# Turned keys of two of four score chunks: loaded from HBM, or turned on TensorE

## The reference

```python
x1 = layernorm(modality1, ln1_g, ln1_b)
x2 = layernorm(modality2, ln2_g, ln2_b)     # the context
q = x1 @ Wq + bq
k = x2 @ Wk + bk
v = x2 @ Wv + bv
scores = jnp.einsum('bqe,bke->bqk', q, k) * scaling
attn = jax.nn.softmax(scores, axis=-1)
ctx = jnp.einsum('bqk,bke->bqe', attn, v)
return ctx @ Wo + bo
```

## Time and profile before

| | us |
|---|---|
| median of 3 executions | 670.63 (665.77 to 671.51) |
| the profiled execution | 672.1 |
| its span, first to last instruction | 670.4 |
| TensorE busy | 606.7 (91%) |
| VectorE busy | 410.6 (61%) |
| ScalarE busy | 260.2 (39%) |
| GpSimd busy | 195.8 (29%) |
| cross attention, from the first turned key to the last weighted tile | 44 to 314 |

### The profile page before, as it was taken

One profiled execution on the slowest core, in us unless ns is written; L12 is line 12 of the kernel. 1 busy time (PEld: TensorE's weight loads), 2 busy tenths in 40 slices (PEclk: granted clock), 3 DMA queues, 4 the chain that ended last, 5 costly groups with the idle time before them and its releaser, 6 DMA issues.

```text
span 670.4 us, 13550 instructions
## 1 busy us (share of the span) xinstructions
PE 606.7 (91%) x5333; PEld 385.4 (57%) x5333; DVE 410.6 (61%) x1004; ACT 260.2 (39%) x627; POOL 195.8 (29%) x259
## 2 busy tenths in 40 slices
PE   5999979999999999998768799999999899998777
PEld 4655445545555555543537395866758585675545
DVE  3974588787778679725567481735548282645522
ACT  0322343757566543532112251533515162351412
POOL 0323387696867775630000000101010000101010
PEclk8999999999999999999788799999999999999879
DMA  8953455464777554729042303021030303012000
GB/s 293 368 184 118 148 201 162 136 189 154 238 237 259 160 190 155 245 107 365 20 115 106 96 1 96 18 80 33 23 88 2 95 18 95 19 56 57 1 17 17
DMA packets 46175, 83.11 MB, mean 124 GB/s; under 512 B 19472, under 2 KB 22048, under 8 KB 44064
## 3 DMA queue, kind: packets, MB, share of 16 engines
q1 hardware_dynamic: 46112, 82.24, 37.7%
HBM read 71.75 MB, written 10.49 MB: 123 GB/s over the span
## 4 chain that ended last, share of the span: by engine, by line
PE 55%; issue 29%; DVE 7%; ACT 4%; POOL 2%; DMA 1%; SPq 0%; DVEq 0%; POOLq 0%; ACTq 0%
PE u_ps L816 10%; PE s_ps L790 9%; PE bank L772 6%; PE bank L878 4%; PE s_ps L772 3%; PE bank L958 2%; PE s_ps L683 2%; ACT area L551 2%; PE u_ps L934 2%; PE bank L988 2%; PE max_ps L958 2%; PE s_ps L716 2%; PE bank L965 1%; DVE area L1318 1%; PE bank L905 1%
## 5 line engine op out<-in xcount | busy, mean ns | idle before, releaser
L461 POOL TENSOR_SCALAR area<-area 128x384 f32<-128x384 f32 (+1 forms) x160 | 106.7, 678 | 10.3 <-POOL area L454 10.3
L1052 DVE BATCH_NORM_STATS2 area<-area 128x6 f32<-128x384 f32 (+1 forms) x208 | 104.0, 541 | 0.0
L551 ACT COPY area<-bank 128x384 f32<-128x384 f32 (+1 forms) x139 | 61.7, 480 | 68.9 <-PE bank L772 68.8
L454 POOL TENSOR_TENSOR area<-area,minus_half 128x4 f32<-128x4 f32 (+1 forms) x56 | 57.1, 1020 | 82.0 <-DVE area L1061 81.5
L816 PE MATMUL u_ps<-area,yT_all 128*64 128x384 f32 (+1 forms) x416 | 78.6, 499 | 0.0
L497 POOL TENSOR_TENSOR area<-area,minus_half 128x1 f32<-128x1 f32 x8 | 4.3, 538 | 242.4 <-DVE area L1312 242.4
L772 PE MATMUL bank<-ident_f,area 128*128 128x128 f32 (+1 forms) x417 | 63.3, 275 | 3.9 <-ACT area L551 2.5
L790 PE MATMUL s_ps<-area 128*64 128x512 f32 x288 | 66.0, 594 | 0.0
L772 PEld LDWEIGHTS bank<-ident_f,area 128*128 128x128 f32 (+1 forms) x417 | 45.1, 141 | 28.4 <-issue 17.6
L934 PE MATMUL u_ps<-area 128*128 128x512 f16 x256 | 60.7, 387 | 0.0
L1152 DVE TENSOR_REDUCE area<-s_ps 128x1 f32<-128x512 f32 x24 | 16.6, 690 | 56.2 <-PE s_ps L790 56.2
(11 more groups left out here) (173 smaller groups left out, 1033.0 us busy)
## 6 DMA issues: line engine op xcount, KB each, us to landing
area<-in_ctx_dram SPq DMA_DIRECT2D x96, 384.0 KB, 3.9
area<-in_L_ffn_W_turned_dram SPq DMA_DIRECT2D x16, 1024.0 KB, 7.9
skew<-area SPq DMA_DIRECT2D x8, 1024.0 KB, 3.9
area<-skew SPq DMA_DIRECT2D x16, 256.0 KB, 4.6
x_sb<-in_x_dram SPq DMA_DIRECT2D x8, 256.0 KB, 9.0
out_dram<-area SPq DMA_DIRECT2D x8, 256.0 KB, 2.0
area<-in_ctx_dram SPq DMA_DIRECT2D x16, 97.5 KB
area<-n_L_xattn_Wq_turned_dram SPq DMA_DIRECT2D x1, 1024.0 KB, 6.9
```

Of the source, the lines that this page charges most:

```text
L454: pool.tensor_tensor(rs[b][:, sl], ve[b][:, sl], minus_half[:, 0:n], ALU.pow).then_inc(s["rstd_ready"], 1)
L461: pool.tensor_scalar(raw[b][0:m, u, j, :], raw[b][0:m, u, j, :], negmu[b][0:m, i:i + 1], rs[b][0:m, i:i + 1], ALU.add, ALU.mult).then_inc( ...
L551: act.copy(xT[c % 2][:, u, :, (j % CH) * P:(j % CH) * P + m], tbank[i % 3][:, 0:KC * P].rearrange("p (c k) -> p c k", c=KC)[:, :, 0:m]).th ...
L1052: dve.bn_stats(st[b][0:m, stat_at(u, j), :], raw[b][0:m, u, j, :]).then_inc(s["key_stats_done"], 1)
```

## The change

The host lays out a second copy of the context, `ctx_turned`: for each batch 384 rows (width) of 1024 keys, those of chunks 1 and 2, not normalised. `load_given` brings one chunk of both batches into `xT`, 1.57 MB in 2 DMAs; chunk 2's waits for the same pair's chunk 0 to be scored, whose buffer it takes, chunk 1's for the previous pair's chunk 1. Tiles 4 to 11 are not turned and not copied. The statistics and the normalising of `raw` stay. The mean is dealt with by centring `a_sb` over the width once (`mean` on TensorE, `centre` on VectorE, in pair 0); the reciprocal deviation of each key is spread over the 64 query rows of its batch by `spread_factors` (8 matmuls with the identity), copied to SBUF by `factors_out`, and multiplied onto the scores in PSUM in the same instruction that takes the maximum. The third turning bank becomes the bank of the factors; two banks are left for turning. The tail has its own buffer. The factors live in the buffer of `fb2`, whose load moves behind the last maximum. The `xvo` groups of pair 0 move two tiles later, behind two `mean` groups.

```diff
+    GIVEN = (1, 2)
+    TURNED = [j for j in range(NJ) if j // CH not in GIVEN]
-        yw, _ = carve(at - 2 * KC * CH * P * 4, [P, D])
+        yw = fb2
+        xT_tail, at = carve(at, [P, 2, KC, TAIL])
+        factors = fb2
-        EXTRA |= {KC + i: ("xvo", i) for i in range(XVO_ROW + 1)}
+        EXTRA |= {KC + h: ("mean", h) for h in range(2)}
+        EXTRA |= {KC + 2 + i: ("xvo", i) for i in range(XVO_ROW + 1)}
-        tbank = [bank[0], bank[1], s_ps[:, 1536:2048]]
+        tbank = [bank[0], bank[1]]
+        factors_bank = s_ps[:, 1536:2048]
+        def slot(ch):
+            return xT_tail if ch == NCH - 1 else xT[ch % 2]
 # SyncE
+            def load_given(p, ch):
+                at_least(sp, s["chunk_scored"], NCH * (p - 1) + 2 if ch == 1 else NCH * p + 1)
+                i = GIVEN.index(ch)
+                for u in range(2):
+                    sp.dma_start(xT[ch % 2][:, u, :, :], A["ctx_turned"][2 * p + u].rearrange("(c d) k -> d c k", d=P)[:, :, i * CH * P:(i + 1) * CH * P]
+                                 ).then_inc(given_loaded[i], 16)
             for k in range(NL):
                 load_pair(0, k)
+            load_given(0, 1)
...
-            for k in range(NL):
+            for k in range(3):
                 load_pair(1, k)
+            load_given(0, 2)
+            for k in range(3, NL):
+                load_pair(1, k)
+            load_given(1, 1)
...
+            load_given(1, 2)
             for p in range(2, NP):
                 for k in range(NL):
                     load_next(p, k)
+                    if k == 2:
+                        load_given(p, 1)
                     if p in (4, 5) and k in (2, 5):
                         load_for_sum(2 * p - 4 + (k - 2) // 3)
+                load_given(p, 2)
...
+            sp.wait_ge(s["chunk_max"], NCH * NP)
+            sp.dma_start(fb2, A["L0_ffn_b2"].partition_broadcast(P)).then_inc(s["fb2_loaded"], 16)
 # ScalarE
-                at_least(act, s["chunk_scored"], c - 1)
+                at_least(act, s["chunk_scored"], NCH * (p - 1) + 3 if j < FT else NCH * p)
+            def factors_out(p, ch):
+                i = len(GIVEN) * p + GIVEN.index(ch)
+                act.wait_ge(s["factors_ps"], i + 1)
+                at_least(act, s["chunk_max"], NCH * p + 2 if ch == GIVEN[1] else NCH * (p - 1) + 3)
+                act.copy(factors, factors_bank).then_inc(s["factors_copied"], 1)
...
-                            evacuate(p, j)
+                            if j in TURNED:
+                                evacuate(p, j)
...
+                    if p < NP and b in (3, 5):
+                        factors_out(p, GIVEN[(b - 3) // 2])
                     if 0 <= q < NP and b in (1, 3, 5, 6):
                         pt_out(q, (1, 3, 5, 6).index(b))
 # TensorE
+                elif kind == "mean":
+                    pe.wait_ge(s["a_ready"], KC + i + 2)
+                    for c in range(KC):
+                        ins = pe.matmul(dst[:, :], ones_f[:, :], a_sb[:, c, i * 512:(i + 1) * 512], start=(c == 0), stop=(c == KC - 1))
+                    ins.then_inc(s["mean_ps"], 1)
...
-                    at_least(pe, s["turned_copied"], i - 2)
+                    at_least(pe, s["turned_copied"], i - 1)
+            def spread_factors(p, ch):
+                i = len(GIVEN) * p + GIVEN.index(ch)
+                if i == 0:
+                    pe.wait_ge(s["cq_sums"], NT)
+                pe.wait_ge(s["rstd_ready"], NB * p + 2 * ch + 2)
+                at_least(pe, s["factors_copied"], i)
+                for j in range(CH):
+                    for u in range(2):
+                        at = stat_at(u, CH * ch + j)
+                        ins = pe.matmul(factors_bank[u * L:(u + 1) * L, j * P:(j + 1) * P], rs[p % 2][:, at:at + 1].to_broadcast([P, L]),
+                                        ident_f[:, :], start=True, stop=True)
+                ins.then_inc(s["factors_ps"], 1)
...
-                            turn(p, j)
+                            if j in TURNED:
+                                turn(p, j)
...
+                        if b in (3, 5):
+                            spread_factors(p, GIVEN[(b - 3) // 2])
 # VectorE
+            def centre(h, src):
+                dve.wait_ge(s["mean_ps"], h + 1)
+                for c in range(KC):
+                    dve.scalar_tensor_tensor(out=a_sb[:, c, h * 512:(h + 1) * 512], in0=src[:, :], scalar=-1.0 / DC, in1=a_sb[:, c, h * 512:(h + 1) * 512],
+                                             op0=ALU.mult, op1=ALU.add).then_inc(s["a_centred"], 1)
...
-                dve.tensor_reduce(mx[:, ch:ch + 1], score_of(ch), AX.X, ALU.max).then_inc(s["chunk_max"], 1)
+                if ch in GIVEN:
+                    dve.wait_ge(s["factors_copied"], len(GIVEN) * p + GIVEN.index(ch) + 1)
+                    dve.tensor_tensor_reduce(score_of(ch), score_of(ch), factors, 1.0, -3.0e38, ALU.mult, ALU.max, mx[:, ch:ch + 1]).then_inc(s["chunk_max"], 1)
+                else:
+                    dve.tensor_reduce(mx[:, ch:ch + 1], score_of(ch), AX.X, ALU.max).then_inc(s["chunk_max"], 1)
```

The host part:

```diff
+    laid["ctx_turned"] = given["ctx_768"][:, :keys * P, :].reshape(-1, P, keys, given["ctx_768"].shape[2])[:, :, 4:12, :].transpose(0, 3, 2, 1).reshape(
+        given["ctx_768"].shape[0], given["ctx_768"].shape[2], 8 * P)
```

More of the change, by code:

```diff
@@ L251, in build_program @@
         raw_loaded = [[sem(f"raw_loaded{b}{k}") for k in range(NL)] for b in range(2)]
+        given_loaded = [sem(f"given_loaded{c}") for c in GIVEN]
         x_loaded = [sem(f"x_loaded{h}") for h in range(2)]
@@ L373, in _ @@
                 sp.dma_start(relT[h * DH:(h + 1) * DH, :], A["L0_attn_rel_emb_turned"][:, first_rel:first_rel + REL]).then_inc(s["rows_loaded"], 16)
-            for dst, key in ((xbo, "xattn_bo"), (abo, "attn_bo"), (fb2, "ffn_b2")):
+            for dst, key in ((xbo, "xattn_bo"), (abo, "attn_bo")):
                 sp.dma_start(dst, A["L0_" + key].partition_broadcast(P)).then_inc(s["rows_loaded"], 16)
+            load_given(1, 2)
             for p in range(2, NP):
@@ L542, in evacuate @@
             def evacuate(p, j):
-                c, m = NCH * p + j // CH, P if j < FT else TAIL
-                if c == 1:
+                m = P if j < FT else TAIL
+                if p == 0 and j == TURNED[1]:
                     act.wait_ge(s["cq_sums"], NT)
-                at_least(act, s["chunk_scored"], c - 1)
+                at_least(act, s["chunk_scored"], NCH * (p - 1) + 3 if j < FT else NCH * p)
                 for u in range(2):
-                    i = 2 * (NJ * p + j) + u
+                    i = 2 * (len(TURNED) * p + TURNED.index(j)) + u
                     act.wait_ge(s["key_turned"], i + 1)
-                    act.copy(xT[c % 2][:, u, :, (j % CH) * P:(j % CH) * P + m],
-                             tbank[i % 3][:, 0:KC * P].rearrange("p (c k) -> p c k", c=KC)[:, :, 0:m]).then_inc(s["turned_copied"], 1)
+                    act.copy(slot(j // CH)[:, u, :, (j % CH) * P:(j % CH) * P + m],
+                             tbank[i % 2][:, 0:KC * P].rearrange("p (c k) -> p c k", c=KC)[:, :, 0:m]).then_inc(s["turned_copied"], 1)
+            def factors_out(p, ch):
[3 more added lines that the diff above has]
+                act.copy(factors, factors_bank).then_inc(s["factors_copied"], 1)
             def exps(q, part):
@@ L786, in scores @@
                     pe.wait_ge(s["xvo_taken"], WO_OUT + XVO_ROW)
-                pe.wait_ge(s["turned_copied"], 2 * (NJ * p + min(CH * (ch + 1), NJ)))
+                if ch in GIVEN:
+                    pe.wait_ge(given_loaded[GIVEN.index(ch)], 32 * (p + 1))
+                else:
+                    pe.wait_ge(s["turned_copied"], 2 * len(TURNED) * p + (2 * CH if ch == 0 else 2 * len(TURNED)))
                 for c in range(KC):
@@ L1238, in _ @@
                             weights(1, EXTRA[j][1], (u_ps, max_ps)[j % 2])
+                        if p == 0 and j in EXTRA and EXTRA[j][0] == "mean":
+                            centre(EXTRA[j][1], (u_ps, max_ps)[j % 2])
                     if p == SMALL_AT and b == 4:
@@ L1403 @@
     laid["L0_attn_rel_emb_turned"] = turned(given["L0_attn_rel_emb"][::-1])
+    keys = given["ctx_768"].shape[1] // P
+    laid["ctx_turned"] = given["ctx_768"][:, :keys * P, :].reshape(-1, P, keys, given["ctx_768"].shape[2])[:, :, 4:12, :].transpose(0, 3, 2, 1).reshape(
+        given["ctx_768"].shape[0], given["ctx_768"].shape[2], 8 * P)
     laid["columns"] = turned(_np.concatenate([given["L0_" + name].reshape(-1, P) for name in
```

24 lines of the change are left out of this document (12 added, 12 removed).

## The result

| | before | after |
|---|---|---|
| median of the executions | 669.70 us (665.77 to 671.51) | 681.03 us (676.61 to 682.55) |
| ratio | | 1.0166 [1.0098, 1.0234] |
| the profiled execution | 672.1 | 680.11 |
| its span | 670.4 | 678.4 |
| its mean TensorE clock | 0.959 | 0.945 |

I had forecast 655.5 us, in a range of 646 to 668.

What follows compares the result with a forecast made beforehand. TensorE was taken to bound each pair (29.69 of 30.20 us busy). Six periods falling from 30.2 to 28.0 give 13.2, plus 3.0 in pair 7, less 1.1 in pair 0: 15.1 us off, so 655.5 us, range 646 to 668.

Steps and rivals of the forecast that it cites:

- Work on TensorE: Cross-attention pairs: 6.6 us of turning removed, about 1.0 us of spreading added in each of chunks 1 and 2.
- rival 2: Spreading in each pair costs its upper bound of 1.9 us; period 29.1, about 665 us, no change; chance 0.14.
- the lost cover: Before the turned context, removing tiles 4 and 5 exposes TensorE's wait for ScalarE's copy, so A shrinks only 0.4 us.
- The load delays VectorE: Next pair's tile 0 lands at S0 + 7.8 behind the turned load; VectorE waits 2.4 us in pairs 1 to 6.
- The chain behind the wait: After VectorE's wait: chunk 1's maximum at S0 + 9.3, then factor copy, then third probability copy done at 11.2.
- Idle 0.75 us: TensorE, arriving at 10.5 after the tail tile, idles 0.75 us for ScalarE's third probability copy.
- No clock term: TensorE's clock was full at 25.1 of 29 us busy, so nothing was added for a slower clock.
- The first (no delay, 648.6): The turned load in SyncE's queue delays nothing; period 26.85, 648.6 us; chance 0.18.
- The third (half rate, 681 us): Turned load at half rate or less makes VectorE's loop the bound; 669 us at 200 GB/s, 681 at 160; chance 0.12.

Runs made afterwards that it cites:

- e1_order: Changed kernel with the next pair's tiles 0 and 1 requested ahead of chunk 2's turned load: 654.73 us, 0.9767 of the kernel before.
- e2_act_first: Changed kernel with ScalarE's probability copy put ahead of its factor copy: 680.38 us, 1.0147 of the kernel before.
- e8_spread_xvo: Changed kernel with tiles 0 and 1 ahead of the turned load, probability copy ahead of factor copy, pair 0's xvo groups spread over later tiles: 651.3 us.
- e12_half_bias: Changed kernel with chunk 2's turned load halved from pair 1 on and GpSimd's bias additions moved behind the pair loop: 661.79 us, 0.99 of before.
- e4_filler: Changed kernel with 20 identity transposes put into TensorE's idle time in each of pairs 1 to 5: 672.81 us, 1.0034 of before.
- e13_weights_apart: Changed kernel with both orders (loads, ScalarE copies) swapped, bias additions late, xvo spread, third turning bank, two weight pieces moved into pair 3: 645.98 us.
- e5_half: Changed kernel with chunk 2's turned load cut to 256 of 512 columns from pair 1 on: 681.88 us, 1.0196 of the kernel before.

## Why the prediction was wrong, step by step

- **Work on TensorE: right.** Spreading takes 1.04 us, step 0.98 (I took 1.0; rival 2, 1.9, fell). The second turned tile of a block waits 0.39 us for one of the two banks (0.37). The turned context waits 0.68 for ScalarE, as the lost cover said. Chunk 0 to chunk 1 is 6.8 us of TensorE against 7.0, pair 7 gave 3.1 us against 3.0, pair 0 cost 1.6 against 1.1.
- **The load delays VectorE: right, and mis-sized.** I had tile 0 at S0 + 7.8. It landed at S0 + 9.5 (request at 166.3, 7.8 us to landing) and the wait is 3.91 us, not 2.4. The rate was not the error: from 167.0 on the queues moved 394 GB/s, where I had taken 393.

```profile
164.85:174.10 9.25, 9.25 (x76) 4.78 (x72) 5.28 (x18) 3.25 (x6) 6.62 (x10) 1.00 0.87 315
...
167.00:174.10 7.10, 7.10 (x54) 3.32 (x50) 3.14 (x13) 1.98 (x4) 5.64 (x8) 1.00 1.02 394
```

  From the request of the turned load (164.85) to the landing of tile 0 (174.1) that is 2.91 MB, and the turned load with tiles 0 and 1 is 2.36 MB. The other 0.55 MB can only belong to the tile requests behind, which were being served while tile 0 was incomplete; at 394 GB/s it takes 1.4 us, nearly the whole miss of 1.5. I had let the queue finish one load before it began the next. This is an estimate from the bytes; no run isolates it. The Trainium skill (DMA: Bandwidth & Descriptors, section Bandwidth) states about 358 GB/s per core on the HBM side; here the trace does not agree, with 394 over 7 us.
- **The chain behind the wait: right in order, missing a collision.** I had the maximum at S0 + 9.3; it came at S0 + 11.56: 1.5 from the load, 0.5 from `own_norm` under GpSimd's additions (1.00 instead of 0.47), 0.2 not accounted for. I had looked at GpSimd only for its sum (22.8 of 28 us) and not for what its 2.5 us of additions do to a VectorE instruction beside them. In this pair they end at 176.07 and `own_norm` at 176.28:

```profile
173.58 2.49 POOL L503 TENSOR_TENSOR x_sb<-x_sb,area 128x512 f32<-128x512 f32 x2
```

- **Idle 0.75 us: wrong, 3.2, and the first step that failed.** The maximum late by 2.3 passes on in full, since nothing on the chain has slack. With pair 6, where TensorE idles 4.84 us behind small reductions that I had not looked at, this is 15.7 us over the six pairs.
- **"No clock term": wrong, and the second step that failed.** I argued from a window with TensorE busy 25.1 of 29 us at clock 1.00. That was an average, and its longest single idle stretch was 1.46 us, half of what my own chain came to make:

```profile
88.89 0.55 PE L772 MATMUL s_ps<-ident_f,area 128*128 128x128 f32 x3 [1.46 <-DVE area L1146]
```

  What the engine did before the clock fell is one stretch of idle time. In the cross attention of all the kernels here, behind each stretch of 2.41 us and more it went to half speed. Shorter ones went either way: half speed behind 1.40 (e1_order) and 2.01 to 2.12 (e2_act_first), full speed behind 1.40 (e8_spread_xvo), 1.46 (before), 2.15 (e12_half_bias) and 2.17 (pair 1 of after). I had a priced idle stretch in my own chain and asked only for its length. Some 12.4 us in the trace, 8 by e4_filler for pairs 1 to 5.
- **Rivals.** The first (no delay, 648.6) is about what e1_order tests: 654.7, since TensorE and VectorE then wait for each other and most periods stay at 28 us or more. With its collisions and the banks mended (e13_weights_apart) three of six periods are 26.2, the others 26.8 to 28.0. The third (half rate, 681 us) names the measured time, but by luck: the turned load ran at full rate, 394 GB/s. Its form, VectorE's loop as the bound, isn't seen either: VectorE was busy under 23 of each 29 us.
- **Range and chances.** The lower and upper ends came from the price of the load and of the spreading. Nothing in it stood for an idle stretch longer than the 0.75 us, or for what one does to TensorE afterwards, so 13 us above the upper end was outside every case.

## What to carry to other kernels

When a change makes TensorE wait once a round, price the wait twice: its length, and the groups behind it at half clock. A trace in which the clock stayed behind much shorter stretches is no reason to leave the second price out. A new load belongs behind whatever the next stage wants first in the same queue, even when both fit the period; here that was a difference of 26 us. And when removing one cause gives nothing, look at what took up the time gained before calling it innocent: e5_half alone would have cleared the load, wrongly.

## What the runs showed of the hardware

- **Half clock after a short wait.** Idle stretches of 2.41 to 3.70 us ahead of a weighted group were followed each time by 1.2 GHz for about 3 to 7 us of work (a weighted group of 1.51 us takes 2.83), which costs 1.4 to 2.9 us in the pairs measured. Between 1.40 and 2.30 us it went either way. 20 transposes in the gap, 2.35 us of them, kept 2.4 GHz and made the kernel 8 us faster.
- **GpSimd's additions stop some VectorE instructions entirely.** While GpSimd adds two 128x512 f32 tiles (2.49 us), a VectorE `tensor_scalar` with operands in SBUF ends only when both are done: 0.47 became 1.94 to 3.10 us, 0.17 became 2.73. The statistics of a tile beside the same additions took their usual time (after, 141.51, 1.02 us for two). The Trainium skill (SBUF — State Buffer, section SBUF: two separate sides) says that the two engines hold a shared port pair as an exclusive lock and that the loser fully blocks. The trace agrees; it adds that VectorE did not get in between two back-to-back additions.
- **Loads in one queue overlap.** The two requests of tiles 0 and 1 behind the turned load landed 7.2 and 7.8 us after they were made, where those of the kernel before took 3.4 and 3.9. The turned load ahead of them makes most of that; but by the estimate above about 0.55 MB of the requests behind them had moved too by then.
